# A four-layer windowed transformer kernel: the last steps of a phase and the first of the next issued in one interleaved order, a new VectorE order in layer 3, and a first load in two halves

## What is computed

```python
h = layernorm(x) ; h = roll(h, -3) ; windows of 49 tokens
q, k, v = h @ qkv_w + qkv_b
a = softmax(q @ k.T * scale + relative_bias + mask)
x = x + roll_back((a @ v) @ proj_w + proj_b)          # attention
h = gelu(layernorm(x) @ w1 + b1)                      # MLP, 96 -> 384 -> 96
x = x + h @ w2 + b2
```

## Time and profile before

| what | value |
|---|---|
| time, median of 3 runs | 9033.19 us (9016.27 to 9047.32) |
| profiled execution: its own time | 9030.85 us |
| profiled execution: span | 9029.0 us |
| mean granted clock of TensorE | 0.968 |
| PE busy | 8243.7 us (91%) |
| DVE busy | 6143.6 us (68%) |
| POOL busy | 5357.4 us (59%) |
| ACT busy | 4966.9 us (55%) |

### The profile page before, as it was taken

One profiled execution on the slowest core, in us unless ns is written; L12 is line 12 of the kernel. 1 busy time (PEld: TensorE's weight loads), 2 busy tenths in 40 slices (PEclk: granted clock), 3 DMA queues, 4 the chain that ended last, 5 costly groups with the idle time before them and its releaser, 6 DMA issues.

```text
span 9029.0 us, 315506 instructions
## 1 busy us (share of the span) xinstructions
PE 8243.7 (91%) x111468; PEld 6122.2 (68%) x111468; DVE 6143.6 (68%) x18728; ACT 4966.9 (55%) x8608; POOL 5357.4 (59%) x6448
## 2 busy tenths in 40 slices
PE   1999999998899999999899999999989999999986
PEld 0667767766677777776667677776666677767765
DVE  2776767766676776766667677675666767667665
ACT  0765747544574664745457375573546647466453
POOL 4865646555685555645568465564656746556454
PEclk8999999999999999999999999999998999999998
DMA  2100010000011010000001101000000100000001
GB/s 36 22 14 8 15 25 15 8 13 10 9 21 29 13 24 17 14 4 19 5 14 21 25 15 29 10 15 4 19 1 17 24 21 15 6 13 12 8 15 22
DMA packets 598544, 142.12 MB, mean 16 GB/s; under 512 B 597379, under 2 KB 598024, under 8 KB 598111
## 3 DMA queue, kind: packets, MB, share of 16 engines
q1 hardware_dynamic: 579204, 132.41, 7.4%
q10 hardware_dynamic: 14027, 3.47, 0.3%
q0 software_dynamic: 4880, 0.71, 0.1%
HBM read 31.68 MB, written 19.27 MB: 6 GB/s over the span
## 4 chain that ended last, share of the span: by engine, by line
PE 46%; issue 20%; DVE 14%; POOL 10%; ACT 3%; DVEq 3%; ACTq 1%; POOLq 1%; DMA 0%
PE ps L747 8%; PE ps L789 7%; PE ps L835 6%; PE ps L735 5%; PE ps L806 4%; PE ps L711 4%; PE ps L754 4%; DVE bst L854 3%; DVE xn L973 2%; PE ps L774 2%; POOL S L509 2%; DVE S L1013 2%; POOL G L495 2%; PE ps L766 2%; DVE agg L862 2%
## 5 line engine op out<-in xcount | busy, mean ns | idle before, releaser
L509 POOL TENSOR_TENSOR S<-S,mx 113x588 f32<-113x588 f32 (+1 forms) x2048 | 2065.5, 1009 | 1706.2 <-DVE mx L1015 1702.1
L632 ACT ACTIVATE PT<-ps 98x588 f32<-98x588 f32 (+1 forms) x2048 | 1182.6, 577 | 1236.5 <-PE ps L789 1229.9
L747 PEld LDWEIGHTS ps<-Vbd,PT 98*49 98x49 f32 x40960 | 1132.8, 127 | 698.7 <-issue 669.6
L1013 DVE TENSOR_TENSOR S<-ps,bias 113x588 f32<-113x588 f32 (+1 forms) x1536 | 963.5, 627 | 872.6 <-PE ps L735 872.6
L747 PE MATMUL ps<-Vbd,PT 98*49 98x18 f32 (+1 forms) x40960 | 1346.5, 203 | 196.6 <-DVE Ot L1027 108.1
L1015 DVE TENSOR_REDUCE mx<-S 113x12 f32<-113x588 f32 (+1 forms) x2048 | 1359.8, 664 | 70.6
L789 PE MATMUL ps<-ident,S 113*98 113x113 f32 x10240 | 1365.9, 265 | 28.7 <-ACT S L615 28.3
L789 PEld LDWEIGHTS ps<-ident,S 113*98 113x98 f32 x10240 | 1054.7, 130 | 470.3 <-issue 370.6
L806 PEld LDWEIGHTS ps<-w,G 128*98 128x98 f32 x12288 | 1161.0, 169 | 162.4 <-issue 91.1
L615 ACT ACTIVATE S<-S 113x588 f32<-113x588 f32 (+1 forms) x2048 | 1241.0, 606 | 45.2 <-POOL S L509 39.6
L806 PE MATMUL ps<-w,G 128*98 128x96 f32 (+1 forms) x12288 | 1160.6, 252 | 4.7 <-DVE x L1066 4.7
(11 more groups left out here) (91 smaller groups left out, 10460.4 us busy)
## 6 DMA issues: line engine op xcount, KB each, us to landing
Vbd<-Vd SPq DMA_DIRECT2D x1536, 41.3 KB
Vbd<-Vd SPq DMA_DIRECT2D x512, 38.3 KB
mask<-L_conv_mask_matrix_dram SPq DMA_DIRECT2D x256, 37.5 KB
x<-x_dram SPq DMA_DIRECT2D x56, 84.0 KB
out_dram<-x SPq DMA_DIRECT2D x48, 84.0 KB
x<-x_dram SPq DMA_DIRECT2D x234, 10.5 KB
out_dram<-x SPq DMA_DIRECT2D x228, 10.5 KB
out_dram<-x SPq DMA_DIRECT2D x180, 18.4 KB
```

The source lines that it names most:

```text
L509: pool.tensor_tensor(v, v, m, ALU.subtract).then_inc(a_sub, 1)
L632: act.activation(PT[:, (s + 3) % 4, 0:blocks, :, :].rearrange("p (b t) w n -> p b (t w) n", b=banks), PTps[:, PT_BANK[l] - 3:PT_BANK[l] - ...
L747: last = pe.matmul(Ops[ROW2 * w:ROW2 * w + N, p, b, :].rearrange("p (a n) -> p a n", a=2), PT[:, p, b, w, :], v, start=True, stop=True)
L1013: dve.tensor_tensor(dst, scores, b, ALU.add).then_inc(a_bi, 1)
```

## The change

Three parts.

1. `quad_steps` is no longer called for whole phases, except in SP. `all_layers` runs the loops and, at the seam MLP of layer l-1 to attention of layer l, and at the seam attention to MLP of layers 1 to 3, issues the last steps of the one and the first steps of the other in one fixed order, the same on PE, DVE, ACT and POOL. Layer 0's attention-to-MLP seam and the seam between groups are as before. The early quads use other PSUM banks (`turned_at`, `keys_at`, `queries_at`), `bst` and `agg` have four slots in place of two, and PE has new waits for `m_res` and `a_res`. The `busy` matmuls of layers 1 to 3 go, but for three in attention step 0. DVE's wait for all 32 rstd is split: half before MLP step -2, all before step 3.
2. Layer 3's MLP on DVE: `xn4` and the next group's statistics come first, then the wait for `l_pow` and L1066.
3. The first `x` is loaded by halves on semaphores of their own, 312 DMAs in place of 228. DVE takes its statistics before it waits for the constants. The weights are loaded by three queues: layers 0 and 3 by SP, 1 by ACT after its bias tables, 2 by POOL.

```diff
+        def mlp_into_attention(of_mlp, mlp, of_att, attend):
+            of_mlp(mlp, NQ - 2)
+            of_att(attend, -2)
+            of_mlp(mlp, NQ - 1)
+            of_att(attend, -1, slots=(0, 1))
+            of_mlp(mlp, NQ)
+            of_att(attend, -1, slots=(2, 3))
+            of_mlp(mlp, NQ + 1)
+            for i in range(4):
+                of_att(attend, i)
+        def attention_into_mlp(of_att, attend, of_mlp, mlp):
+            of_att(attend, NQ - 2)
+            of_att(attend, NQ - 1)
+            of_mlp(mlp, -2)
+            of_att(attend, NQ, slots=(0, 1, 2))
+            of_mlp(mlp, -1)
+            of_att(attend, NQ, slots=(3,))
+            of_mlp(mlp, 0)
+            of_att(attend, NQ + 1)
+            of_att(attend, NQ + 2)
+            for i in range(1, 4):
+                of_mlp(mlp, i)
+        def early(l, i):
+            return l > 0 and i.static and i.index < 0
+        def turned_at(l, i):
+            bank = (4 if i.index == -1 else 0) if early(l, i) else X_BANK
+        def keys_at(l, i):      # bank 1 if early, else X_BANK
+        def queries_at(l, i):   # bank 0 if early, else Z_BANK
...
-            tokens(sp, 0, False, s_x, turn=0, turns=2)
+            tokens(sp, 0, False, s_x0, 0, IMGS // 2, turn=0, turns=2)
+            tokens(sp, 0, False, s_x, IMGS // 2, IMGS, turn=0, turns=2)
+            for l in (0, 3):
+                load_weights(sp, l, load)
...
 PE attend
-                            if i.static and i.index < 0:
+                            if l == 0 and i.static and i.index < 0:
                                 busy(0, 2 if s in (0, 3) else 1)
-                            if i.static and i.index == 0 and s < 2:
+                            if l == 0 and i.static and i.index == 0 and s < 2:
                                 busy(4, 2)
+                            if l > 0 and i.static and i.index == 0 and s == 1:
+                                busy(4, 3)
                             if s == 0 and on(1):
                                 wait(a_ht, i + 1)
+                                if l > 0 and i.static and i.index == 0:
+                                    pe.wait_ge(m_res, base)
                             if s == 2 and on(1):
                                 wait(a_qe, i + 1)
+                                if early(l, i):
+                                    pe.wait_ge(m_res, base - 1)
 PE mlp
+                        if l > 0 and p.static and p.index == 0:
+                            pe.wait_ge(a_res, base + NQ)
-                        if i.static and i.index < 0:
+                        if l == 0 and i.static and i.index < 0:
                             busy(5, 3)
...
 DVE
+            dve.wait_ge(s_x0, 16 * HALF_DMAS)
+            quad_steps(dve, 0, load_stats, 2, 0, NQ // 2)
+            dve.wait_ge(s_x, 16 * HALF_DMAS)
+            quad_steps(dve, 0, load_stats, 2, NQ // 2, NQ)
+            dve.wait_ge(s_memset, 1)
+            dve.wait_ge(s_const, n_const[0])
+            dve.wait_ge(s_const2, n_const2[0])
 DVE mlp
+                        if l > 0 and i.static and i.index == -2:
+                            dve.wait_ge(s_rstd, (g * RSTD_PHASES + 2 * l - 1) * NQ + NQ // 2)
+                        if l > 0 and i.static and i.index == 3:
+                            dve.wait_ge(s_rstd, (g * RSTD_PHASES + 2 * l) * NQ)
+                        if on(2):
+                            ... xn4 of quad i + 2 (L973), moved up
+                        if last_layer and on(0):
+                            ... all_stats of the next group, moved up
                         if last_layer and on(-2):
                             p = i - 2
                             dve.wait_ge(l_pow, lbase + i.index - 1)
                             ... L1066
-                        if on(2):
-                            ... xn4
-                        if last_layer and on(0):
-                            ... all_stats of the next group
```

More of the change, by code:

```diff
@@ L238, in build, with quad_steps @@
         RSTD_PHASES = 2 * LAYERS - 2
-        def quad_steps(eng, base, body, full=4):
+        def quad_steps(eng, base, body, full=4, first=0, last=NQ):
             skew, unroll = 2, 2
             pbase = base * QUAD if isinstance(base, int) else eng.snap(base * QUAD)
-            for i in range(-skew, full):
-                body(Unit(0, base, i, 0, pbase), i, lambda d: 0 <= i + d < NQ)
-            with eng.Fori(full, NQ - skew - unroll + 1, unroll) as r:
+            for i in range(first - skew, first + full):
+                body(Unit(0, base, i, 0, pbase), i, lambda d: first <= i + d < last)
+            with eng.Fori(first + full, last - skew - unroll + 1, unroll) as r:
                 n = eng.snap(base + r)
@@ L253, in quad_steps, with held_steps, step @@
                 nc.disable_value_cache = True
-            for i in range(NQ - skew, NQ + skew + 1):
-                body(Unit(0, base, i, 0, pbase), i, lambda d: 0 <= i + d < NQ)
+            for i in range(last - skew, last + skew + 1):
+                body(Unit(0, base, i, 0, pbase), i, lambda d: first <= i + d < last)
+        def held_steps(eng, base):
+            pbase = eng.snap(base * QUAD)
+            def step(body, i, **more):
+                body(Unit(0, base, i, 0, pbase), i, lambda d: 0 <= i + d < NQ, **more)
+            return step
@@ new lines, in rolled_steps @@
+        def rolled_steps(eng, base, body):
+            first, last, unroll = 4, NQ - 2, 2
+            pbase = eng.snap(base * QUAD)
+            with eng.Fori(first, last - unroll + 1, unroll) as r:
+                n = eng.snap(base + r)
+                r4 = eng.snap(r * QUAD)
+                n4 = eng.snap(pbase + r4)
+                nc.disable_value_cache = False
+                for j in range(unroll):
+                    body(Unit(r, n, j, r4, n4), j, lambda d: True)
+                nc.disable_value_cache = True
@@ L996, in attend @@
                                 low = dve.snap(low, min_val=0, max_val=2)
-                        for s in range(QUAD):
+                        for s in slots:
                             e = s % 2
```

233 lines of the change are left out of this document (127 added, 106 removed).

## The result

| | before | after |
|---|---|---|
| median, beside each other on one chip | 9040.26 us (9016.27 to 9054.35, 4 runs) | 8787.8 us (8726.97 to 8886.33, 4 runs) |
| profiled execution, span | 9029.0 us | 8884.5 us |
| mean granted clock there | 0.968 | 0.955 |

The ratio is 0.9711, 95% interval 0.967 to 0.9752. Medians here are of all runs; ratios and intervals leave out runs more than 1.5% above the fastest of their kernel. The change makes the kernel 2.9% faster, by 252 us and not by the 415 of the forecast. The time is 28 us past the upper end of the range.

The account below looks back on a forecast made before the run. PE was 91% busy, but the start, the seams and layer 3's MLP, not bound by PE, left time to win: 48 + 138 + 96 + 133 = 415 us off 9031, about 8615 us, range 8500 to 8760.

Parts of the forecast that it names:

- The start: Before the first group: statistics run before the constants land at 135.5, L946 at 157 us; 48 us saved (37 to 56).
- Layer 3: Layer 3's MLP: new DVE order cuts the step from 6.675 to 5.6 us (at most 6.2 to 6.3); 133 us (47 to 183).
- layer 3 gives nothing: Layer 3's MLP: DVE and POOL block each other until the step is again 6.7 us; total 8749 us, chance 0.10.
- the old ring: Layer 3's MLP step before: variance on DVE, power on POOL, add on DVE, `xn4`, statistics, variance; 6.675 us a step.
- that rule at its worst: Layer 3's MLP: each small DVE operation waits out a POOL operation, the gain goes; total 8749 us instead of 8615.
- The seams: 12 MLP-to-attention seams at 11.5 us each, 138 us (84 to 168); 12 attention-to-MLP seams at 8 us, 96 us (48 to 142).
- the other seam, from attention to the MLP: 12 seams: 26.5 us shrinks to 18.5, filler gone, about 4 us of waits left; 8 us each, 96 us (48 to 142).
- if the half clock of this place stays: Attention-to-MLP seam, lower end: half clock lasts through the first `w1` product, so only 4 us a seam, 48 in all.
- it would be wrong if the loops themselves changed: Sign of a wrong prediction: the loops themselves change; attention steps in the loop were expected unchanged.
- the clock falls at the seams: 24 seams without filler each have another 10 us at half clock, adding 120 us; total 8735 us, chance 0.09.
- Slower than before: Clock stays at half long after each seam, 37 us behind each of 24; total 9060 us, chance 0.03.

Follow-up runs that it names:

- POOL paced: POOL's `x` + `c2` in layer 3's MLP held until VectorE wrote next quad's `xn`: in after 8694.83 us; in before with layer 3's new order 8887.88 us.
- The filler at the drain: Kernel after plus six 128 x 512 filler products in the last attention steps of layers 1 to 3: 8817.85 us, ratio 0.9673 to before.
- pacing and drain filler: Kernel after with both POOL's `x` + `c2` wait in layer 3's MLP and six filler products in the last attention steps: 8629.77 us, ratio 0.9516 to before.
- the five start products: Five more wide filler products at each attention start, layers 1 to 3: in after alone 8775.58 us; with pacing and drain filler 8613.7 us.

## Why the prediction was wrong

**The start: right.** 48 us forecast, 47.6 measured. DVE is released by the last constant at 135.23, against 135.5. That this is so close is partly luck: ACT's queue ran 90.25 + 32.73 us for `x` and bias tables, where 96.2 + 28.2 was counted, and the two errors nearly cancel. L946 (now L1046) stands at 156.57 against 157.

**Layer 3: the step that failed.** The sum took a step of 5.6 us, "nearer the lower bound, since POOL is busy 90.02 of 150 us here and two collisions in every step are the most that this leaves likely". POOL's mean busy share says nothing about where its operations fall. The new order starts `xn4` at the moment when the variance is done, and that same moment releases POOL's row of four operations. The collision is therefore in nearly every step (120 of 128 quads), and more than one of the four `xn4` operations can meet it: in the step before the one shown, the second takes 1.08 us and the third 1.05. The step came to 6.7 us by the matmul count, 1.1 above the forecast and past its upper end of 6.3. The term of 133 us was worth 30 to 50. That the collision was it is shown: with POOL paced, `xn4` takes 1.40 us again and the step is 5.7 in the new kernel and 5.6 in the old one. The first rival, *layer 3 gives nothing*, had the mechanism and the sign against the forecast, at a chance of 0.10; its 8749 was closer. The argument against it, "the old ring contained the same operations", was wrong: it contained them in another phase to each other.

The Trainium skill's page "SBUF — State Buffer", section "Who interferes with whom", has the pair of shared ports as an exclusive lock for a whole instruction. The trace agrees for the large operations: `xn4` (2.93 us for four) ends with L645, and without L638 beside it takes 1.40. It does not for L652, an operation of 1.02 us on 98 x 4: `xn4` operations of 0.33 us run inside it. The forecast weighed that rule at its worst and then priced it by the mean; what is left, 30 to 50 of 133 us, is nearer the worst case.

**The seams: mechanism right, size off.** The chain from quad 30's statistics over POOL's rstd to `xn` gave 6.05 us where 6 to 6.5 was forecast, with 1.49 us of wait. Yet a seam of this kind is worth 80/12 = 6.7 us and not 11.5. The window of the earlier trace rows shows 12.7 us of gain, but the sum left out what the seam costs beside the window. Attention's first transpose now stands ahead of it, with one more wait on POOL's `xn` (0.54 and 1.53 us at 775.35): from the `w2` of quad 29 to that of quad 30 it is 6.15 us and not 4.08. And attention behind the seam is longer, from first to last scores 364.7, 363.2 and 251.4 us in layers 1 to 3, where the kernel with this seam as before has 361.9 to 362.6, 361.9 and 250.2. These two make 3 to 5 of the 6 us.

At the other seam, from attention to the MLP, the filler is gone and only 0.7 of 24 us are idle, better than forecast, but the granted clock is 0.54 where it was 0.81: 22 us, not 18.5. It is the case of the forecast's lower end, "if the half clock of this place stays". One seam where it did not fall took 14.3 us. The filler at the drain removes the fall and shows that this was it.

A term that the sum did not have at all is the MLP loop of layer 1. In layer 1 the stretch from first `w2` to the end of quad 30 takes 146.2 to 147.9 us and not 141.3. Of this 2.1 us are the moved transpose and its wait, 1.2 us the first quad, which starts at half clock, and 3 us the loop step of 4.79 us in place of 4.68. DVE stands idle 0.72 us ahead of every second `xn4`, where it was 0.58, and PE waits 0.55 us for it and not 0.32. The forecast held that it would be wrong if the loops themselves changed; this one did, by a little. Neither the seams nor the new order did this: the kernel before with the new start alone has a step of 4.79 us as well. (Layer 0's step went the other way, from 4.74 to 4.68.) Why is open; it is some 6 us in all.

**The clock.** The second rival, *the clock falls at the seams*, came true at one kind of seam, and cost some 7 us in each of layers 1 and 2 (21.7 against 14.3). *Slower than before* did not come true, but its mechanism, the clock at half long after a seam with PE 100% busy, is what spreads the runs of after. A stretch of 126 us costs 421.5 - 368.7 = 53 us (first to last scores of layer 0 with and without it). The forecast gave this rival 0.03, and noted that in the earlier trace rows it came "without an idle gap to explain it". How much is at stake the removed products show: with none, three and eight products at the start of attention, the kernel with pacing and drain filler has 9358, 8630 and 8614 us. They are not the whole cause: with 16 such products the kernel before with the new start still had a stretch of 406 us. The Trainium skill, "TensorE: Matmul & The Clock Gate", section "Why this matters for your kernels", advises to pad thin matmuls or else the clock swings. No run here pads a matmul; wide products of no use beside the thin ones did help, as the three times above show. The page's swing is not what is seen here, though, where the clock stays down for 27 to 410 us.

Rivals come one at a time, and the results of two of them came at once: 8615 with layer 3's loss and the seams' is 8771, over the range's upper end with no more half-clock time than before had. The range was built as if one of them would happen.

One reading of the forecast was off too: PE's idle time in a step of layer 3's MLP, "1.3 us" in the second rival, is 1.1 by the earlier trace rows (24.2 us in 22.5 steps). Nothing in the sum hangs on it.

**What stays open.** Why a half-clock stretch ends when it does; why attention at half clock, with PE fully busy, is not given the full clock; whether the five start products exclude the stretches or only make them rarer (two profiles with them have none in layers 1 to 3); why 16 products in the old place did not; the changed MLP loop steps of layers 0 and 1; and the 20223.41 us execution. Some 6 us of the 12.7 that a seam into attention saves come back beside it, of which 1 to 3 are not pinned down.

## What to carry to other kernels

When a wait is taken away, look at what the freed engine now starts beside, at that moment, on an engine that can hold it up; a mean busy share can't price it, and one wait that separates them may be worth more than the reorder (93 us here). What a window of the trace loses in length is no saving if work or waits only move ahead of it or behind it: count them at their new place. And filler is not always waste, though it computes nothing: in one kernel three wide products per phase carried 728 us, so before filler is removed each place of it is to be tested by itself.

## What the hardware showed unexpectedly

- A VectorE `TENSOR_SCALAR` of 98 x 96, 329 ns in the median, lasted up to 2031 ns in after (1173 in before, 1183 paced). That one began at 4384.14, with L638, and ended with L645 behind it: two large GpSimd operations back to back were waited out by one instruction. GpSimd's 98 x 4 power operation, 1.02 us long, did not delay it.
- At a granted clock of 0.50, this kernel's attention keeps PE 100% busy and stays there for 27 to 126 us, or for some 400 us, in the profiles of these kernels.
- Adding work sped PE up: with nothing else changed, the kernel with the three start products has 72 matmuls more in its trace than the one without (111156 and 111084) and 746.5 us less PE busy time (8039.5 and 8786.0).

The forms of `xn4` in after and in before (duration min/median/max in ns), for the first of these:

```profile
L1073 DVE TENSOR_SCALAR xn<-x,mv,rstd x1536: 315/329/2031, 1152.8 to 8815.7; 98x96 f32 x192
```
```profile
L973 DVE TENSOR_SCALAR xn<-x,mv,rstd x1536: 315/329/1173, 1170.4 to 8960.3; 98x96 f32 x192
```
